# Output projection: o of the second group loaded first, its rounding on ScalarE, four transposes two rows later

## What is computed

```python
def _attention(x, W_qkv, W_out, b_out):
    ...
    out = jnp.einsum('bhqk,bkhd->bqhd', attn, v).reshape(Bq, Tq, INNER)
    return out @ W_out + b_out
...
x = x + g_msa * _attention(_modulate(_layernorm(x), sh_msa, sc_msa), W_qkv, W_out, b_out)
x = x + g_mlp * _ff(_modulate(_layernorm(x), sh_mlp, sc_mlp), W1, b1, W2, b2)
```

## Time and profile before

| | before |
|---|---|
| median of 3 runs | 3134.89 us (3132.53 to 3136.94) |
| profiled execution | 3134.77 us, its span 3132.9 us |
| TensorE matmuls busy | 3056.4 us, 98% |
| VectorE | 1860.1 us, 59% |
| ScalarE | 1337.5 us, 43% |
| GpSimd | 809.0 us, 26% |
| granted TensorE clock, mean | 0.99 of full speed |
| output projection, first to last product | 2211.5 to 2405.7 us |

### The profile page before, as it was taken

The page is one execution under the profiler, slowest core; times in us unless marked ns, Lnnn a source line. Parts: engine busy times, 40 slices in busy tenths (PEclk is TensorE's granted clock), DMA queues, the critical chain, the costliest instruction groups (busy, mean ns, idle before and its releaser), DMA issues.

```text
span 3132.9 us, 61847 instructions
## 1 busy us (share of the span) xinstructions
PE 3056.4 (98%) x24696; PEld 2437.2 (78%) x24696; DVE 1860.1 (59%) x2752; ACT 1337.5 (43%) x2784; POOL 809.0 (26%) x529
## 2 busy tenths in 40 slices
PE   8979999999999899999999999999899999999998
PEld 5968997888888677777777777777678888888887
DVE  4358983222222488888888888888586434333332
ACT  2146663222222377777777777777101211111111
POOL 1001113000000244443444434446455101111110
PEclk9989999999999999999999999999999999999999
DMA  4554322333333333333333333333464001010100
GB/s 143 170 176 175 112 78 104 108 101 107 118 110 115 101 110 82 96 89 100 85 83 94 91 99 86 83 92 93 165 244 176 1 28 34 28 35 27 34 14 14
DMA packets 198362, 297.61 MB, mean 95 GB/s; under 512 B 27840, under 2 KB 105664, under 8 KB 196054
## 3 DMA queue, kind: packets, MB, share of 16 engines
q1 hardware_dynamic: 187088, 284.93, 29.0%
q0 software_dynamic: 1728, 6.29, 0.6%
q10 hardware_dynamic: 9296, 2.77, 0.4%
HBM read 190.44 MB, written 103.49 MB: 94 GB/s over the span
## 4 chain that ended last, share of the span: by engine, by line
PE 63%; DVE 2%; DMA 1%; issue 0%; ACT 0%; POOL 0%; SPq 0%; DVEq 0%; ACTq 0%; POOLq 0%
PE b_po L1344 15%; PE b_ps L1315 12%; PE d_pf L1805 11%; PE d_po L1816 11%; PE b_tp_act L1327 7%; PE c_po L1576 4%; PE b_tp_dve L1327 3%; DMA c_ot<-o_t 1%; DVE c_ol L1594 0%; PE d_pt L1797 0%; DVE c_oh L1592 0%; DVE o_first_rest L1594 0%; DVE norm_st L840 0%; DVE o_first_high L1592 0%; POOL d_y L1746 0%
## 5 line engine op out<-in xcount | busy, mean ns | idle before, releaser
L1374 DVE TENSOR_REDUCE b_nm<-b_ps 128x1 f32<-128x1024 f32 x512 | 601.9, 1216 | 18.3 <-PE b_ps L1315 5.0
L1283 ACT ACTIVATE b_p<-b_ps,b_nm 128x1024 f32<-128x1024 f32 x512 | 564.6, 1112 | 29.5 <-DVE b_nm L1374 29.5
L1344 PE MATMUL b_po<-b_pt,b_v 128*64 128x256 f32 x4096 | 498.3, 385 | 0.8 <-DVE b_pt L1394 0.8
L1288 ACT ACTIVATE b_pt<-b_tp_act 128x512 f32<-128x512 f32 x512 | 307.9, 601 | 306.4 <-PE b_tp_dve L1327 306.4
L1394 DVE COPY b_pt<-b_tp_dve 128x512 f32<-128x512 f32 x512 | 351.0, 686 | 117.9 <-PE b_tp_dve L1327 117.8
L1327 PEld LDWEIGHTS b_tp_act<-ident,b_p 64*128 64x128 f32 x4096 | 312.1, 138 | 118.6 <-issue 100.8
L1344 PEld LDWEIGHTS b_po<-b_pt,b_v 128*64 128x64 f32 x4096 | 272.1, 136 | 128.5 <-ACT b_pt L1288 0.9
L1327 PE MATMUL b_tp_act<-ident,b_p 64*128 64x64 f32 x4096 | 348.2, 225 | 2.4 <-issue 2.4
L1327 PE MATMUL b_tp_dve<-ident,b_p 64*128 64x64 f32 x4096 | 348.6, 225 | 0.0
L1780 ACT ACTIVATE d_ge<-d_pf,b_t 128x512 f32<-128x512 f32 x128 | 88.2, 689 | 576.6 <-PE d_pf L1805 576.6
L1327 PEld LDWEIGHTS b_tp_dve<-ident,b_p 64*128 64x128 f32 x4096 | 312.4, 138 | 14.6
(11 more groups left out here) (279 smaller groups left out, 6202.0 us busy)
## 6 DMA issues: line engine op xcount, KB each, us to landing
b_raw_q<-q_t SPq DMA_DIRECT2D x124, 256.0 KB, 4.3
q_t<-p_qk SPq DMA_DIRECT2D x64, 256.0 KB, 2.0
k_t<-p_qk SPq DMA_DIRECT2D x64, 256.0 KB, 2.0
v_n<-p_vs SPq DMA_DIRECT2D x32, 512.0 KB, 3.2
b_v<-v_n SPq DMA_DIRECT2D x32, 512.0 KB, 3.9
b_raw_k<-k_t SPq DMA_DIRECT2D x124, 128.0 KB, 4.2
c_ot<-o_t SPq DMA_DIRECT2D x7, 2048.0 KB, 7.9
a_x<-x SPq DMA_DIRECT2D x32, 256.0 KB, 3.3
```

Source lines behind the costliest of these rows:

```text
L1283: act.activation(pr[k % 4][:], ps[k % 2][:], ACT.Exp, bias=nm[:, k % 4:k % 4 + 1], accum_out=rs[:, n:n + 1]).then_inc(exp_done, 1)
L1288: act.activation(dst, src, ACT.Copy).then_inc(t_out[0], 1)
L1344: mm = pe.matmul(po[rows, (blk % 2) * 2 * P:(blk % 2 + 1) * 2 * P], vt[u][:, kc, rows], pt[blk % 2][h][:, kc, :], start=(kc == 0), stop=(k ...
L1374: dve.tensor_reduce(nm[:, k % 4:k % 4 + 1], ps[k % 2][:], axis=AX.X, op=ALU.max, negate=True).then_inc(max_done, 1)
```

## The change

Three things. SyncE issues load_o(1) ahead of the first gate, bias and y. The casts of the splits (high parts, 7 groups x 8) leave VectorE's list and stand in ScalarE's, where `round_o(g+1)` opens group g, ahead of the modulations that fall into that group; from the second on it waits also until the products that read the buffer are done. VectorE keeps the subtractions, each waiting for its cast. And T_AT and X_AT are two rows later each.

```diff
-    T_AT = (6, 8, 10, 12)
-    X_AT = (8, 10, 12, 14)
+    T_AT = (8, 10, 12, 14)
+    X_AT = (10, 12, 14, 16)
...
+            load_o(1)
             load_gate(0)
             load_y(0)
-            load_o(1)
             load_y(1)
...
-            for n in range(GT):
+            def round_o(g):
+                act.wait_ge(o_in, 16 * g)
+                if g >= 2:
+                    act.wait_ge(m_done, (g - 1) * GT)
+                for c in range(KO):
+                    act.copy(oh[g % 2][:, c, :], ot[:, c, :]).then_inc(rounded, 1)
+
+            def modulate(n):
                 act.wait_ge(zt_done, n + 1)
...
+            for g in range(NG):
+                if g + 1 < NG:
+                    round_o(g + 1)
+                for n in range(GT):
+                    if T_AT[n] // GT == g:
+                        modulate(n)
...
             def split(g):
-                dve.wait_ge(o_in, 16 * g)
                 for c in range(KO):
-                    dve.tensor_copy(oh[g % 2][:, c, :], ot[:, c, :]).then_inc(rounded, 1)
                     dve.wait_ge(rounded, (g - 1) * KO + c + 1)
```

## The result

The changed kernel takes 3126.2 us in the median of 8 runs (3125.34 to 3128.62) against 3133.39 us of the kernel before (8 runs, 3131.11 to 3137.74): the ratio is 0.9975, with a 95% interval of 0.9964 to 0.9986. It is faster by 7.2 us. The forecast was 3124.7 us with a range of 3117.0 to 3131.0. The profiled execution took 3126.95 us, its span 3125.1 us. (In the kernel before, the function of the stage begins at L1424, as the printed code shows, not at L1399.)

What follows compares the result with a forecast made beforehand. TensorE's waits between output projection and feed-forward, with clock and refilling, lose 17.9 us; all go, but a new wait costs 7.8, so 10.1 us are gained: 3134.8 - 10.1 = 3124.7 us, range 3117.0 to 3131.0.

Steps and rivals of the forecast that it cites:

- The bound: TensorE, output projection to feed-forward: 194.2 us for 176.2 us of work, so at most 17.9 us can be won.
- The gap at group 1: TensorE's 1.5 us wait for the last subtraction of split(1) goes, also at the worst.
- the term for split(1): VectorE's first split takes 5.8 us instead of 8.5, ending at 2228.5, at worst 2231.5; TensorE wants it at 2233.4.
- The wait for z: First transposes: the 7.9 us gap goes with its clock cost; z complete at 2253.1, asked for at 2260.6.
- The second transposes: After row 10: o(3) lands at 2263.7, modulation behind ScalarE's casts ready at 2269.3, wanted at 2272.0; margin 2.7 us.
- the forecast's sign that c_po runs without a gap through row 14: TensorE's output projection: no gap from row 0 through row 14 would show the prediction right.
- The wait at the fourth transposes: After row 14, c_xm(2) stands behind split(4) and o(4), landing at 2290.1: new wait of 5.3 us, 7.8 in all.
- Sharing between w1 and o(4): Rival on the DMA engines: w1 and o(4) share them, the new wait does not come, 3116.9 us; chance 0.12.
- The loads do not come forward: Rival on loads: gates, y and o contend; o(2), z and o(3) come as late as before, 3132.6 us; chance 0.18.
- not over 1.65: Rival on ScalarE: casts, forecast at 0.5 us, cost over 1.65; at 2.2 us each the kernel takes 3155 us; chance 0.03.
- The later groups: Later groups have slack: a load of 7.9 us and a split of about 8 fit in a group's 21.8 us.

Runs made afterwards that it cites:

- e3: The changed kernel with the second split of c_xm after row 11 and modulations 0 and 2 ahead of ScalarE's casts of groups 3 and 4: 3116.4 us, ratio 0.9945.
- e2: The changed kernel with the second split of c_xm after row 11 instead of 12, so ahead of split(4) on VectorE: 3120.9 us, ratio 0.9958.
- e4: The changed kernel with load_o(1) back behind gate and y, casts still on ScalarE and transposes late: 3125.1 us, ratio 0.9974.
- e1: The changed kernel with the 4 MB load of w1 issued in group 3 instead of group 1: 3117.4 us, ratio 0.9948.
- e8: The kernel before with only load_o(1) moved ahead of gate and y, casts and subtractions on VectorE: 3134.0 us, ratio 1.0003.
- e6: The kernel before with only the casts of the splits moved to ScalarE, old order of loads and old rows: 3120.4 us, ratio 0.9961.
- e7: The changed kernel with GpSimd's adds to y of group 0 waiting until split(1) is done: 3126.0 us, ratio 0.9973.
- e5: The kernel before with only the transposes and splits of c_xm moved two rows later, casts on VectorE: 3135.5 us, ratio 1.0004.

## Why the prediction was right, and where its sizes were off

**The bound.** That 17.9 us could be won, all in this stage, was right to 0.2 us: e3 has a stage of 176.4 where 176.2 were reckoned.

**The gap at group 1** went, as said. But the term for split(1) was mis-sized: 5.8 us, at worst until 2231.5, and the subtractions took 10.4 and ended at 2232.9, with 0.2 us to spare. That the gap went altogether was thin: e2, with the same lists up to there, has 0.6 us of it. The prediction saw that y would land last, at 2226.5 (it was there at 2225.8), and that subtractions stay at 1.67 us beside GpSimd. It did not put the two together in full: y lands in the midst of the split just because o was put first. The Trainium skill (SBUF — State Buffer, Who interferes with whom) says that a VectorE instruction with two SBUF inputs contends with one of GpSimd that reads SBUF, by an exclusive lock on the ports that the two share, while ScalarE waits for nobody. The traces agree in that both sides grow longer and ScalarE's casts do not: eight subtractions take 4.9 us alone and 10.4 beside the adds, the adds 5.0 and 6.6; eight casts on ScalarE take 4.27 us, those that began at 2240.75 beside adds as those at 2267.09 without.

**The wait for z** went, with 7 us in hand (the first of c_z done at about 2253.2, asked for at 2260.4). z was complete at 2255.5 instead of 2253.1, since o(2), issued 4.5 us later than forecast, landed at 2240.75, outside the 2236.4 to 2239 given.

**The second transposes**: ScalarE's queue was named as the place, with a margin of 2.7 us. o(3) landed at 2267.1, not 2263.7, and the margin became a wait of 1.0. Of these 3.4 us 2.4 come from z; the other 1.0 is the load itself, 11.2 us from issue to landing where the forecast took the 10.1 of before. With this wait the forecast's sign that c_po runs without a gap through row 14 failed.

**The wait at the fourth transposes** came where and as it was forecast: split(4), gated, split of c_xm, modulation, from landing to TensorE 2303.34 - 2293.43 = 9.9 us (10.0 forecast). Its size was off since o(4) landed at 2293.4 instead of 2290.1: 7.5 instead of 5.3. y(3) was issued 2.3 us later than forecast (2269.6), and from there to o(4)'s landing were 23.8 us instead of 22.8. The clock gave back a part by luck, 1.5 instead of 2.3: e4 lost 2.0 behind the same wait of 7.5 us. Lost in all 10.5 instead of 7.8, so 7.4 gained in the stage instead of 10.1.

**The rivals.** Sharing between w1 and o(4) was rejected on a row of before, rightly. e1 alone doesn't show it, as w1's bytes would delay o(4) under sharing too. The time from issue to landing does; this is the line of the kernel before (KB, median us to landing):

```profile
w_raw<-w SPq DMA_DIRECT2D x1, 4096.0 KB, 16.0
```

It was 16.2 us in the change. So w1, issued at 2271.08, landed near 2287.3, and o(4), half its size and issued 1.6 us behind it, 6.1 us later (5.4 before). Shared evenly, the smaller one would have landed first; so w1's bytes came first. "The loads do not come forward" had a little truth: o(3) was issued 5.4 us sooner instead of 7.8, and landed 4.4 sooner. ScalarE's casts cost 0.53 us each, not over 1.65. The later groups had their slack, though their splits took 10.4 to 11.5 us beside the adds, not 8: no gap stands behind the fourth transposes.

**What the prediction did not ask** is whether the parts need each other. Each loss of the third part was in its text (a step behind split(4) instead of split(3)), but the sum was only made for the three together. The runs show that the second part wins 11.3 us alone and the others give 3.9 of them back. The intervals of the two ratios overlap (0.9946 to 0.9975 and 0.9964 to 0.9986); what parts them is the stages, 182.9 and 186.8, with the gaps that make them up.

## What to carry to other kernels

When a consumer is moved later to give its input time, look at which transfers now stand ahead of its input in each in-order list: here two rows later was ample for z, and put one step behind the slowest load on two engines at once. Ask of each step whether what it is queued behind waits for a DMA, and order the lists so that nothing ready stands behind something that is not; in the changed kernel that was worth 10 us, with no load moved and no work saved (e3). And a load that is put first makes another one last: see what the late one starts, and whom that collides with.

## What was not expected of the hardware

Beside GpSimd's adds eight subtractions on VectorE cost 5.5 us more (10.4 against 4.9), and the adds 1.6 us more (6.6 against 5.0): both sides pay. One subtraction that meets an add takes 1.67 us instead of 0.69, and a VectorE cast of the same size 1.51 instead of 0.42 (before, at 2245.23).

The clock's price did not grow with the wait. It is what TensorE lost behind a gap, refilling left out:

| TensorE idle, us | kernel | lost in the clock, us |
|---|---|---|
| 3.5 | e8 | 1.6 |
| 3.8 | before | 2.6 |
| 3.8 | e8 | 1.3 |
| 4.0 | e6 | 1.7 |
| 4.2 | e2 | 1.3 |
| 6.2 | e8 | 1.9 |
| 7.4 | e7 | 1.3 |
| 7.5 | the change | 1.5 |
| 7.5 | e4 | 2.0 |
| 7.9 | before | 1.4 |
| 12.1 | e5 | 2.1 |

Each time the granted clock was 0.50 for 2.7 to 5.5 us of TensorE's work behind the gap, and half of that time was lost; behind the idle times of 0.6 to 2.2 us nothing was lost. In e6, and behind the gap of 3.5 us in e8, the clock fell only after TensorE was at work again. So a wait of 4 us costs 5 to 6.5 in all, and one of 7.5 some 9 to 9.7, in this kernel. The same length of wait lost 1.3 and 2.6, or 1.5 and 2.0; what decides between them is not settled by these runs.
